# Two transformer layers on one core: down weights loaded ahead of the next block, GpSimd's bias rows in the projection, VectorE's weight halves in the last batch

## The chip, the cores and the metric

The kernel runs on one core of a Trainium2 chip. The metric is the time of one execution on the device in microseconds, as the median of several runs; less is better. The engines are TensorE (PE, matmul, with its weight loads as PEld), VectorE (DVE), ScalarE (ACT), GpSimd (POOL) and SyncE (SP), which here only issues DMAs. Each has a queue of its own and works it off in order; they wait for each other through semaphores.

## What is computed

Two layers on a residual x of 8 x 112 rows of 512, in fp32. Layer 0, which the change touches:

```python
x = layer_norm(hidden, ln1_w, ln1_b)
q, k, v = heads(x @ q_w + q_b), heads(ctx @ k_w + k_b), heads(ctx @ v_w + v_b)   # 16 heads of 32
attn = softmax(where(mask, q @ k.T / sqrt(32), min))      # 112 x 375 per batch and head
hidden = hidden + (attn @ v) @ cproj_w + cproj_b
out = hidden + gelu(layer_norm(hidden, ln2_w, ln2_b) @ fc_w + fc_b) @ proj_w + proj_b   # 512 -> 2048 -> 512
```

Layer 1 has two cross attentions with 16 heads of 128 and one more key each, and an MLP of the same size. The context has 8 x 375 rows of 512.

## The kernel before, in words

**Precision.** Every fp32 operand of a product is held as two halves, hi (ScalarE or VectorE writes it in fp32r) and lo (the difference, by a subtraction on VectorE or GpSimd). `product` makes three matmuls: hi x hi, hi x lo, lo x hi (lines 1696 to 1698).

**Weights** come in blocks of 512 x 512 in two slots, a and b. `load_block` on SP asks for four columns of 128 into `w_raw`; a column waits until the lo half of the same column of the block before is made (`w_lo`). `split_hi` (ScalarE, L877) makes hi, `split_lo` (L1234 on VectorE, L787 on GpSimd) makes lo. Slot a holds in turn the query weights, the key weights (A_K0) and the MLP's up weights (A_M0, A_M0 + 1, ...); slot b the value weights, the output projection (B_O0), and the MLP's down weights (B_M0, ...).

**Order of layer 0** (`schedule`, the same order on every engine):
- `ln(0)` and `query`: 896 rows are 7 tiles of 128. VectorE measures a row tile (`measure`, bn_stats L1238), normalizes it (`normalized`, L1263), TensorE turns it (`turn_row`, L1706), ScalarE scales it (`scaled`, L892), VectorE makes its halves (`halves`, L1269 and L1271). The query product is eight steps; steps 0 to 3 need the first four row tiles, and row tiles 4, 5 and 6 are turned behind steps 0, 1 and 2 (`later_rows`). Steps 4 to 7 need all seven. ScalarE evicts each step (L932).
- `attend_first`: eight batches, each of four tiles t of 128 columns, which are four heads j. For a tile: key product into ps_k (`key`), its eviction in two halves (`key_hi` L962, `key_lo` L1374), scores of four heads (`score_quad`, L1807), masked maximum (L1391), exp (L972), normalization (L1365, L1368), transpose (`turn`, L1820), eviction (`turned`, L968), weighted sum (`weighted`, L1832). Tile t + 1 is scored while tile t is turned. The parts of the following key and value products stand between the transposes (FILL). GpSimd makes the lo halves of the context for the batch after next (`context_lo`, L809), and then adds the output projection's bias to one row tile of x (`add_bias`, L803), for batches 0 to 6; it waits for nothing else between.
- In the last batch (`final`) there is no following batch. TensorE puts the first output rows (`first_row`) between the transposes; ScalarE makes the hi halves of B_O0 after each exp of tile 0, GpSimd their lo halves, and one column of A_M0 is made after each of tiles 0, 1 and 2. SP asks for A_M0 + 1, all four columns, and then for B_M0.
- `project`: last output rows, second layer norm (`add_y` L1574 adds a product to x). The last column of A_M0 is made here.
- `mlp`, four blocks: `up` in two chunks of four products with GELU (L1197), then `down`. In block 0 ScalarE also makes B_M0's hi halves and the halves of the context by key (L1188), which SP asked for behind B_M0 in `project`.

## Time and profile before

| | us |
|---|---|
| median of 3 runs (2320.42 to 2322.63) | 2320.61 |
| the profiled execution | 2322.78 |
| its span | 2321.0 |
| TensorE busy | 2276.6 (98%) |
| VectorE busy | 1335.5 (58%) |
| ScalarE busy | 1122.4 (48%) |
| GpSimd busy | 362.6 (16%) |
| mean granted TensorE clock, share of full | 0.999 |

A timeline row has the start in us from the span's start, the duration, the engine, line, operation, the tile written <- the tiles read, shapes, and the number of instructions merged into it. A bracket at its end is idle time of the engine just before it, and what ended that. PE's ends are modelled and its matmuls overlap, so a wait is read from the bracket, not from the gap. Layer 0's attention ends at about 297 us, its MLP at about 475 us.

### The profile page before, as it was taken

Reading aid. Unit: us, or ns where it says so; the run is one execution under the profiler, and the core shown is the slowest. Engines: PE = TensorE matmul, PEld = TensorE weight load, DVE = VectorE, ACT = ScalarE, POOL = GpSimd, SP = SyncE. Lnnn points to the kernel's source line nnn. Section 1 sums busy time; section 2 is a strip of 40 time slices with the busy share of each in tenths; the row PEclk is TensorE's granted clock in tenths of the full one; section 3 lists DMA queues with packets and bytes.
Section 4 is the critical chain, followed back from the end, with each engine's and each line's share of the span. In section 5 each row is a group of like instructions: output and inputs, shape, how many; then the busy total and the mean of one; then the engine's idle time right before and its main releaser. Section 6 shows DMA issues by size and latency. Waiting matters only on the chain.

```text
span 2321.0 us, 37085 instructions
## 1 busy us (share of the span) xinstructions
PE 2276.6 (98%) x13091; PEld 2068.1 (89%) x13091; DVE 1335.5 (58%) x3098; ACT 1122.4 (48%) x2468; POOL 362.6 (16%) x731
## 2 busy tenths in 40 slices
PE   7999999999999999999999999999999999999999
PEld 6777778899999999999998899999999999988888
DVE  5888764434655655655654525565565565554743
ACT  5777743344444445444543435445445444453421
POOL 1111045520000100100101210001001001003421
PEclk9999999999999999999999999999999999999999
DMA  6422036585545645654645564555555556444110
GB/s 192 139 90 98 16 117 197 183 251 152 190 144 194 226 168 170 226 190 151 236 144 158 179 190 153 197 177 189 198 197 177 197 190 201 173 156 136 58 55 32
DMA packets 255224, 376.25 MB, mean 162 GB/s; under 512 B 90302, under 2 KB 210514, under 8 KB 255042
## 3 DMA queue, kind: packets, MB, share of 16 engines
q1 hardware_dynamic: 255042, 373.87, 47.9%
q8 instruction: 108, 1.77, 0.3%
q14 instruction: 74, 0.61, 0.1%
HBM read 315.77 MB, written 58.05 MB: 161 GB/s over the span
## 4 chain that ended last, share of the span: by engine, by line
PE 92%; DVE 3%; ACT 2%; issue 2%; DMA 1%; SPq 0%; DVEq 0%; ACTq 0%
PE ps_k L1696 10%; PE ps_k L1697 10%; PE ps_k L1698 10%; PE ps_o L1696 9%; PE ps_o L1698 8%; PE ps_o L1697 8%; PE ps_v L1696 6%; PE ps_v L1698 6%; PE ps_v L1697 6%; PE ps_s L1696 4%; PE ps_s L1698 4%; PE ps_s L1697 4%; PE ps_t L1882 3%; PE ps_t L1820 2%; PE ps_o L1832 1%
## 5 line engine op out<-in xcount | busy, mean ns | idle before, releaser
L1696 PE MATMUL ps_k<-cs_hi,w_a_hi 128*128 128x376 f32 x1136 | 383.8, 338 | 2.8 <-DVE k_lo L1374 1.5
L1697 PE MATMUL ps_k<-cs_lo,w_a_hi 128*128 128x376 f32 x1136 | 379.5, 334 | 0.0
L1698 PE MATMUL ps_k<-cs_hi,w_a_lo 128*128 128x376 f32 x1136 | 378.5, 333 | 0.0
L1088 ACT ACTIVATE prob<-ps_s,row_columns 112x376 f32<-112x376 f32 x256 | 147.2, 575 | 303.5 <-DVE row_columns L1471 303.5
L829 POOL CAST k_hi<-xk_hi 128x1 fp32r<-128x1 f32 x256 | 47.0, 183 | 1232.4 <-PE ps_s L1698 1232.4
L1696 PEld LDWEIGHTS ps_k<-cs_hi,w_a_hi 128*128 128x128 f32 x1136 | 213.4, 188 | 4.7 <-issue 4.0
L1697 PEld LDWEIGHTS ps_k<-cs_lo,w_a_hi 128*128 128x128 f32 x1136 | 213.7, 188 | 0.5
L1698 PEld LDWEIGHTS ps_k<-cs_hi,w_a_lo 128*128 128x128 f32 x1136 | 213.6, 188 | 0.0
L1465 DVE SCALAR_TENSOR_TENSOR k_lo<-ps_k,col_b,k_hi 128x375 fp32r<-128x375 f32 x252 | 152.8, 606 | 75.0 <-ACT k_hi L1057 69.3
L1057 ACT ACTIVATE k_hi<-ps_k,col_b 128x375 fp32r<-128x375 f32 x252 | 143.9, 571 | 86.4 <-PE ps_k L1698 85.3
L1365 DVE RECIPROCAL row_columns<-row_columns 112x1 f32<-112x1 f32 x384 | 62.6, 163 | 197.9 <-ACT prob L1088 188.3
L1368 DVE TENSOR_SCALAR prob<-prob,row_columns 112x375 f32<-112x375 f32 x384 | 170.7, 445 | 4.5
L787 POOL TENSOR_TENSOR w_b_lo<-w_raw_b,w_b_hi 128x512 fp32r<-128x512 f32 x84 | 112.4, 1365 | 389.5 <-ACT w_b_hi L877 389.5
L1493 DVE TENSOR_TENSOR sums_lo<-ps_o,sums_hi 128x448 fp32r<-128x448 f32 x128 | 79.9, 624 | 131.6 <-ACT sums_hi L1071 131.6
L1471 DVE TENSOR_REDUCE row_columns<-ps_s 112x1 f32<-112x376 f32 x256 | 138.3, 540 | 8.0 <-PE ps_s L1698 8.0
L1698 PE MATMUL ps_v<-pt_hi,ckd_lo 128*128 128x448 f32 (+1 forms) x384 | 141.2, 368 | 0.0
L1696 PE MATMUL ps_v<-pt_hi,ckd_hi 128*128 128x448 f32 (+1 forms) x384 | 140.2, 365 | 0.9 <-DVE pt_lo L1487 0.9
L1698 PE MATMUL ps_o<-pt_hi,ckd_lo 128*128 128x448 f32 (+1 forms) x384 | 140.7, 366 | 0.0
L1696 PE MATMUL ps_o<-pt_hi,ckd_hi 128*128 128x448 f32 (+1 forms) x384 | 140.6, 366 | 0.0
L1697 PE MATMUL ps_v<-pt_lo,ckd_hi 128*128 128x448 f32 (+1 forms) x384 | 140.3, 365 | 0.0
L1697 PE MATMUL ps_o<-pt_lo,ckd_hi 128*128 128x448 f32 (+1 forms) x384 | 140.2, 365 | 0.0
L1493 DVE TENSOR_TENSOR sums_lo<-ps_v,sums_hi 128x448 fp32r<-128x448 f32 x128 | 80.0, 625 | 101.2 <-ACT sums_hi L1071 100.8
(275 smaller groups left out, 5712.3 us busy)
## 6 DMA issues: line engine op xcount, KB each, us to landing
ckd_hi<-context_by_key_halves SPq DMA_DIRECT2D x64, 768.0 KB, 4.4
ckd_lo<-context_by_key_halves SPq DMA_DIRECT2D x64, 768.0 KB, 6.2
cs_hi<-context_halves SPq DMA_DIRECT2D x64, 752.0 KB, 6.1
cs_lo<-context_halves SPq DMA_DIRECT2D x64, 752.0 KB, 7.8
w_raw_b<-in_blocks_b SPq DMA_DIRECT2D x104, 256.0 KB, 4.3
w_raw_a<-in_blocks_a SPq DMA_DIRECT2D x104, 256.0 KB, 4.8
q<-q_scratch SPq DMA_DIRECT2D x72, 224.0 KB, 6.0
extra<-extra_probability SPq DMA_DIRECT2D x16, 896.0 KB, 5.2
```

The lines of the kernel that those rows point to most:

```text
L787: pool.tensor_tensor(w[slot][1][:, :, part], w_raw[slot][:, :, part], w[slot][0][:, :, part], ALU.subtract).then_inc(w_lo[slot], 1)
L1057: act.activation(k[t % 2][0][:, 0:LK], key_bank(place, t)[:, 0:LK], ACT.Identity, bias=col_b[:, ds(place.column((C_BK0, C_BK1), t), 1)]).t ...
L1088: act.activation(prob[buf][0:LQ, 0:KW], ps_s[buf][0:LQ, 0:KW], ACT.Exp, bias=max_neg[0:LQ, buf:buf + 1], accum_out=prob_sum[0:LQ, buf:buf ...
L1365: dve.reciprocal(prob_rcp[0:LQ, col:col + 1], prob_sum[0:LQ, col:col + 1]).then_inc(s_rcp, 1)
L1368: dve.tensor_scalar(p[0:LQ, 0:LK], p[0:LQ, 0:LK], prob_rcp[0:LQ, col:col + 1], None, ALU.mult).then_inc(s_norm, 1)
L1465: dve.scalar_tensor_tensor(out=k[t % 2][1][:, 0:LK], in0=key_bank(place, t)[:, 0:LK], scalar=col_b[:, ds(place.column((C_BK0, C_BK1), t), 1)],
L1471: dve.tensor_reduce(max_neg[0:LQ, t % 2:t % 2 + 1], ps_s[t % 2][0:LQ, 0:KW], AX_X, ALU.max, negate=True).then_inc(s_max, 1)
L1493: dve.tensor_tensor(sums[1][:, d, cols], ps_c[d % 2][:, 0:HALF], sums[0][:, d, cols], ALU.subtract).then_inc(c_lo, 1)
L1696: pe.matmul(out, w_h, m_h, start=first, stop=False)
L1697: pe.matmul(out, w_h, m_l, start=False, stop=False)
L1698: return pe.matmul(out, w_l, m_h, start=False, stop=last)
L1882: last = pe.transpose(ps_t[buf][0:n, i * LQ:(i + 1) * LQ], prob[buf][0:LQ, k0:k0 + n], ident[0:LQ, 0:LQ])
```

## The change

- `key_bank`: in layer 0, tile 1 of the first batch goes to ps_o[0] in place of ps_k.
- `ln(0)`: GpSimd adds the bias to row tiles 0 to 3 when four row tiles have their halves, and to 4 to 6 when row tile 6 is normalized, and then makes batch 1's context halves. `attend_first` adds none. Row tile 6 is turned behind query step 1; its deviation on ScalarE stands ahead of the first query eviction; VectorE normalizes it ahead of row 4's halves.
- Last batch: the hi halves of B_O0 stand at other places on ScalarE, VectorE makes the lo halves, and the columns of A_M0 are made in tiles 2 and 3.
- `project`: row 6 is added and measured ahead of row 4's halves.
- SP: B_M0 is asked for in the last batch with nothing ahead of it; three columns of A_M0 + 1 stand behind the first context by key, the fourth behind the next bias row.

```diff
+PROJECTION_LOW = {(0, 1): 0, (1, 0): 2, (1, 1): 3}
...
         self.key_ahead = 2 if layer == 0 else 3
-        self.split_slots_b = {(NB - 1, 0): range(4)} if layer == 0 else {}
...
-    def split_columns_b(self, t):
...
-        return self.att.split_slots_b.get((self.b, t), ()) if isinstance(self.b, int) else ()
...
+if not place.att.layer:
+    return ps_o[0] if place.head and place.parity == 0 and t == 1 else ps_k
...
-return place.att.layer and place.head and (t == NT - 1 if place.parity == 0 else t < NT - 1)
+if not place.att.layer:
+    return place.head and place.parity == 0 and t == 1
+return place.head and (t == NT - 1 if place.parity == 0 else t < NT - 1)
...
 if isinstance(norm, int) and norm == 0:
-    return {0: (4,), 1: (5,), 2: (6,)}
+    return {0: (4,), 1: (5, 6)}
...
     sp.sem_inc(sp_waited, 1)
+    if isinstance(e, int) and e == 1:
+        load_block(0, A_M0 + 1, [3])
...
         if place.swap:
-            load_block(0, place.block_a + 2)
...
         load_by_key_raw(0)
+        load_block(0, A_M0 + 1, range(3))
...
+    if isinstance(e, int) and e == 0:
+        pool.wait_ge(bias_in, 16)
+        pool.wait_ge(ln_lo, 4)
+        for r in range(4):
+            add_bias(r)
+        pool.wait_ge(ln_xhat, RT)
+        for r in range(4, RT):
+            add_bias(r)
+        context_lo(Place(ATT0, 0, 0, 0, 1))
+        return
     pool.wait_ge(ln_lo, RT * e + RT)
-    if has_pending(e):
-        split_lo(*pending(e)[0:2])
-    if isinstance(e, int) and e == 0:
-        context_lo(Place(ATT0, 0, 0, 0, 1))
+    split_lo(*pending(e)[0:2])
     pool.wait_ge(bias_in, 16 * e + 16)
-    if has_pending(e):
-        for r in range(RT):
-            add_bias(r)
+    for r in range(RT):
+        add_bias(r)
...
         for t in range(NT):
-            if t == 0 and place.b < RT:
-                add_bias(place.b)
...
                 context_lo(place.after(2))
-            split_lo(1, place.block_b + 1, place.split_columns_b(t))
...
         deviation(0, 5)
+        deviation(0, 6)
...
             scaled(norm, row)
-        if not layer and i == 0:
-            deviation(0, 6)
...
         act.sem_inc(act_waited, 1)
-        act.activation(k[t % 2][0][:], ps_k[:, 0:KW], ACT.Identity,
+        act.activation(k[t % 2][0][:], key_bank(place, t)[:, 0:KW], ACT.Identity,
...
+    def projection_part(place, s):
+        split_hi(1, place.block_b + 1, [s], lambda s: (v_mm, 3 * place.batch + 3))
...
+    def mlp_part(place, s):
+        split_hi(0, place.block_a + 1, [s], lambda s: (k_mm, place.tile + NT))
...
         following = place.key(t + 1)
-        for j in range(SUB0):
-            if not (t == 0 and j == 3):
-                turned(place, t, j)
-            if t == 0 and j == 2:
-                turned(place, t, 3)
-            if following:
-                exp(*following, j)
-            if key_evicted(place, t, j):
-                key_hi(*key_evicted(place, t, j))
-            if t == 0:
-                split_hi(1, place.block_b + 1, (j,), lambda s: (v_mm, 3 * place.batch + 3))
-            if t == NT - 1 and j == 1:
-                deviation(1, 0)
-                deviation(1, 1)
-        if t == NT - 1:
+        turned(place, t, 0)
+        if t == 0:
+            projection_part(place, 0)
+            exp(*following, 0)
+            turned(place, t, 1)
+            exp(*following, 1)
+            turned(place, t, 2)
+            turned(place, t, 3)
+            exp(*following, 2)
+            key_hi(*place.key(t + 2))
+            exp(*following, 3)
+            projection_part(place, 1)
+        if t == 1:
+            projection_part(place, 2)
+            exp(*following, 0)
+            turned(place, t, 1)
+            projection_part(place, 3)
+            exp(*following, 1)
+            turned(place, t, 2)
+            exp(*following, 2)
+            key_hi(*place.key(t + 2))
+            turned(place, t, 3)
+            exp(*following, 3)
+        if t == 2:
+            exp(*following, 0)
+            turned(place, t, 1)
+            exp(*following, 1)
+            mlp_part(place, 0)
+            turned(place, t, 2)
+            exp(*following, 2)
+            turned(place, t, 3)
+            exp(*following, 3)
+            mlp_part(place, 1)
+        if t == 3:
+            mlp_part(place, 2)
+            turned(place, t, 1)
+            deviation(1, 0)
+            deviation(1, 1)
+            turned(place, t, 2)
+            turned(place, t, 3)
...
             output_hi(place, t)
-            if place.split_column(t) is not None and not (place.final and t == NT - 1):
+            if place.split_column(t) is not None and not place.final:
...
         measure_rows((6,))
+        scale_rows((6,))
         halves(0, 4)
-        scale_rows((6,))
...
         dve.wait_ge(k_hi, place.tile + t + 1)
-        dve.scalar_tensor_tensor(out=k[t % 2][1][:], in0=ps_k[:, 0:KW], scalar=col_a[:, C_BK0 + t:C_BK0 + t + 1],
+        dve.scalar_tensor_tensor(out=k[t % 2][1][:], in0=key_bank(place, t)[:, 0:KW], scalar=col_a[:, C_BK0 + t:C_BK0 + t + 1],
...
             measure(1, r)
+        split_lo(0, A_M0, [2])
...
                         key_lo(*place.key(t + 2))
+                if place.final and (t, j) in PROJECTION_LOW:
+                    split_lo(1, place.block_b + 1, [PROJECTION_LOW[t, j]])
+                if place.final and (t, j) == (2, 1):
+                    split_lo(0, place.block_a + 1, [0])
...
                 normalized_0(*following, SUB0 - 1)
+            if place.final and t == 0:
+                split_lo(1, place.block_b + 1, [1])
+            if place.final and t == 2:
+                split_lo(0, place.block_a + 1, [1])
...
             output_lo(place, t)
-            if place.split_column(t) is not None and not (place.final and t == NT - 1):
+            if place.split_column(t) is not None and not place.final:
...
         measure(norm, 5)
+        add_y(6, 0, 0)
+        scale(5)
+        measure(norm, 6)
         halves(norm, 4)
-        scale(5)
-        add_y(6, 0, 0)
-        measure(norm, 6)
+        scale(6)
         split_lo(0, A_M0, [3])
-        scale(6)
...
         if two_key_banks(place, t) and place.parity == 0:
-            pe.wait_ge(q_act, 8 * (4 * place.a + 4) + 6)
+            pe.wait_ge(q_act, 8 * (4 * place.a + 4) + 6 if place.att.layer else 7)
```

## Rows read from the trace of the kernel before

**Rows 1.** The page: busy us (share of the span) x instructions of each engine
```profile
PE 2276.6 (98%) x13091; PEld 2068.1 (89%) x13091; DVE 1335.5 (58%) x3098; ACT 1122.4 (48%) x2468; POOL 362.6 (16%) x731
```

**Rows 2.** Timeline, query projection: start, us, engine, line, operation, count [idle before <-releaser]
```profile
27.03 0.69 DVE L1271 TENSOR_TENSOR act_t_lo<-o,act_t_hi 128x512 fp32r<-128x512 f32 x1
...
29.82 0.55 DVE L1263 TENSOR_SCALAR shared<-x,mean_var,row_columns 128x512 f32<-128x512 f32 x1
...
30.93 0.69 DVE L1238 BATCH_NORM_STATS2 stats<-x 128x6 f32<-128x512 f32 x1
...
31.23 1.50 ACT L892 ACTIVATE o<-ps_t,col_a 128x128 f32<-128x128 f32 x4
...
33.69 0.45 PE L1696 MATMUL ps_o<-act_t_hi,w_a_hi 128*128 128x448 f32 x1
...
40.22 0.47 PE L1696 MATMUL ps_k<-act_t_hi,w_a_hi 128*128 128x448 f32 x1 [1.03 <-DVE act_t_lo L1271]
```

**Rows 3.** Timeline, first MLP block, where GpSimd adds the second bias
```profile
327.60 8.88 POOL L803 TENSOR_TENSOR x<-x,bias_row 128x512 f32<-128x512 f32 x6
...
332.41 1.53 DVE L1648 TENSOR_TENSOR cs_lo<-prob,cs_hi 128x384 fp32r<-128x384 f32 x1
```

**Rows 4.** Timeline, PE at the start of attention
```profile
53.63 0.41 PE L1696 MATMUL ps_k<-cs_hi,w_a_hi 128*128 128x376 f32 x1 [1.49 <-DVE k_lo L1374]
```

**Rows 5.** Timeline, batch 1's last tile and its fellows in other batches
```profile
107.59 3.15 POOL L809 TENSOR_TENSOR cs_lo<-ctx_raw,cs_hi 128x376 fp32r<-128x376 f32 x3
...
110.71 1.28 POOL L803 TENSOR_TENSOR x<-x,bias_row 128x512 f32<-128x512 f32 x1
...
110.98 1.22 DVE L1368 TENSOR_SCALAR prob<-prob,row_columns 112x375 f32<-112x375 f32 x1
...
114.04 0.61 ACT L972 ACTIVATE prob<-prob,row_columns 112x375 f32<-112x375 f32 x1 [1.40 <-DVE row_columns L1391]
...
115.22 0.49 PE L1820 MATMUL ps_t<-ident,prob 112*128 112x112 f32 x3 [0.67 <-ACT shared L968]
...
85.62 0.48 PE L1820 MATMUL ps_t<-ident,prob 112*128 112x112 f32 x3 [1.19 <-ACT shared L968]
...
257.03 0.42 DVE L1368 TENSOR_SCALAR prob<-prob,row_columns 112x375 f32<-112x375 f32 x1
```

**Rows 6.** Timeline, the last batch
```profile
267.10 1.47 DVE L1368 TENSOR_SCALAR prob<-prob,row_columns 112x375 f32<-112x375 f32 x1
...
273.85 0.68 DVE L1234 TENSOR_TENSOR w_a_lo<-w_raw_a,w_a_hi 128x512 fp32r<-128x512 f32 x1
...
269.27 0.79 PE L1832 MATMUL ps_o<-shared,v 128*32 128x112 f32 x24 [1.30 <-ACT shared L968]
...
271.06 0.42 PE L1807 MATMUL ps_s<-k_hi,q 32*112 32x376 f32 x2 [1.00 <-DVE k_lo L1374]
...
276.20 0.49 PE L1820 MATMUL ps_t<-ident,prob 112*128 112x112 f32 x3 [1.52 <-ACT shared L968]
```

**Rows 7.** Timeline, SP's queue and the MLP's first products
```profile
274.55 37.97 SPq L531 DMA_DIRECT2D w_raw_a<-in_blocks_a  x4
...
309.78 0.66 PE L1706 MATMUL ps_t<-ident,shared 128*128 128x128 f32 x4 [0.32 <-DVE shared L1263]
...
313.94 0.47 PE L1696 MATMUL ps_s<-act_t_hi,w_a_hi 128*128 128x512 f32 x1 [0.30 <-ACT prob L1197]
...
322.75 0.63 ACT L1188 ACTIVATE ckd_hi<-ctx_raw 128x512 fp32r<-128x512 f32 x1 [0.74 <-DMA ctx_raw<-in_ctx_by_key]
...
324.10 0.42 PE L1696 MATMUL ps_s<-act_t_hi,w_a_hi 128*128 128x384 f32 x1 [2.34 <-ACT prob L1197]
```

**Rows 8.** Busy us by stretch: PE, PEld, DVE, ACT, POOL, PEclk, DMA share, GB/s
```profile
325.00:326.00 1.00, 1.00 (x5) 1.00 (x4) 0.14 (x1) 1.00 (x3) 1.00 (x1) 0.50 0.62 150
...
325.00:330.00 5.00, 5.00 (x23) 5.00 (x22) 3.38 (x5) 2.60 (x5) 5.00 (x4) 0.70 0.58 163
...
1220.00:1222.00 2.00, 2.00 (x7) 1.78 (x6) 0.00 (x0) 0.32 (x1) 0.00 (x0) 0.50 0.92 330
```

## The prediction

> **What bounds the kernel now.** I read the page's head first: TensorE is busy in 2276.6 us, 98% of the span of 2321.0 [rows 1]. So there are at most 44 us of idle TensorE in the whole kernel, and the change can win only where TensorE waits; work moved between the other engines counts only through such a wait. Next I went down TensorE's timeline from 0 to 560 us and kept the rows that end in a bracket, that is those with idle time ahead of them: 32 rows, some 33 us, of which 10.4 is the first load. For each wait in a stretch that the diff touches I then read VectorE, ScalarE, GpSimd and SP's queue backwards from the releaser, since the bracket names only the last link. Last I looked at the granted clock by stretch: it is 1.00 (2.4 GHz) but for two places, where it is 0.50, the lower level of 1.2 GHz [rows 8]; both stand right behind waits of TensorE.
>
> The profiled execution took 2322.78 us, 2.17 more than the median of 2320.61. I make the sum against the profiled one and come back to the difference.
>
> **1. Key tile 1 of the first batch gets its own bank (gain 1.5).** TensorE waits 1.49 us for the low half of tile 0, only because both tiles use ps_k [rows 4]. With tile 1 in ps_o[0] the product starts at once. The new wait, for the seventh query product's eviction, ends before it, as products 5 to 8 are evicted as they come. Next late is the score of tile 0, which needs the same low half; the 12 matmuls of tile 1's product, some 2 us, now lie above it. The rest of the start hangs on TensorE and moves along. Bounds 1.0 and 1.5.
>
> **2. GpSimd's bias rows leave the batches (gain 4.2).** In batches 0 to 5 there is one wait each before a transpose in the last tile: 1.19 us once and about 0.68 five times [rows 5]. The chain behind the 0.67 is: the context's low halves hold GpSimd until 107.59 + 3.15 = 110.74, a bias row follows at 110.71 for 1.28. VectorE's normalization issued at 110.98 takes 1.22, and the same instruction takes 0.42 in batch 6, where GpSimd is idle. It ends 0.2 behind the end of the bias row. So the maximum that follows, ScalarE's exp (which idles 1.40 for it), the eviction behind the exp and TensorE's transpose are all 0.80 late. Without the row 0.80 goes, and 0.67 of it is TensorE's. Five times 0.67 and 0.83 (0.80 to 0.83 of the 1.19; the rest, 0.36, has other reasons) make 4.2. What is late next is TensorE itself: the eviction ahead of the transpose is then done about 0.1 us before it is wanted, which is thin. The other slowed normalizations lie under the context halves, which stay. Bounds 0 (the 0.1 doesn't hold) and 4.6.
>
> **3. The same rows now run in the projection (loss 1.3).** This is the edit that I am least sure of. GpSimd begins rows 0 to 3 when the fourth row's low half is done, 27.03 + 0.69, and rows 4 to 6 when row 6 is normalized. In that stretch VectorE is on the path: TensorE starts its fifth product at 40.22, after waiting 1.03 for VectorE's last halves [rows 2]. In the other stretch where GpSimd adds a bias, its rows take 8.88 / 6 = 1.48 each, and VectorE's subtraction takes 1.53 [rows 3], against 0.69 for a wider one alone [rows 2]: about one VectorE operation per GpSimd row. First without contention: ScalarE now does row 6's deviation ahead of the first query eviction, so it waits for statistics that start at 30.93 and are aggregated by about 31.95; its scaling of row 4 moves from 31.23 to about 32.85 and ends at 34.35. TensorE turns row 6 one product earlier, where the third product now starts, at 33.69, but that turn waits for row 4's scaling: 0.7 lost, 1.03 won, because the last halves are then done at about 39.0. With contention the normalizations of rows 4 and 5 (29.82 and the next) each wait for the end of a bias row, which puts the statistics of row 6 1.2 later; the turn waits 1.9; and three casts and three subtractions for rows 4 to 6 meet the bias rows 4 to 6. I get the last halves at about 41.4, 1.3 later, and TensorE's fifth product at 41.5 in place of 40.22: a loss of 1.3. Bounds: a gain of 1.0 (nothing is put in), and a loss of 4 (a whole further row of 1.28 ahead of two of the halves). I take 1.3, as rows 3 are the same operations on the same engines.
>
> The Trainium skill says the same of the cause (SBUF — State Buffer, Who interferes with whom): VectorE and GpSimd share one port pair as an exclusive lock, and an instruction with two SBUF inputs or in a 2-port mode is fully blocked. By that rule bn_stats, with one input, would not wait, and edit 3 stays as worked out; by a lock on every VectorE instruction the statistics would wait too and it would come out about 1.3 higher. No row shows statistics beside a GpSimd row. It is the rule that speaks against this edit.
>
> **4. The last batch (gain 0.9).** TensorE waits 1.30, 1.00 and 1.52 there, 3.8 in all [rows 6]. The cause is again GpSimd, which makes four weight halves while VectorE's normalizations take 1.47 (against 0.42 in rows 5). VectorE now makes those halves itself, four at about 0.6 of its queue each (0.68 in rows 6); one more, of the MLP's weights, leaves the first tile. Going through the new order with these durations: ScalarE has one half ahead of its evictions in place of two, so the weighted sum starts at about 268.6 (was 269.27); the third tile's low half is done about 0.4 earlier, scores at 270.65 (was 271.06). Then the fourth weight half is ready only at about 275.5, and the first output row, which now comes up at 274.5, has to wait about 1 us for it; before, it was covered by the wait of 1.52. At the end of tile 1 TensorE is 1.0 ahead. In tiles 2 and 3 one more MLP half comes before the third row's addition; about 0.1 is given back. Bounds 0 and 3.8; a loss is not to be had unless the fourth half is later than 276.4.
>
> **5. Order of rows 5 and 6 ahead of the MLP (gain 0.6).** VectorE now adds row 6 and measures it before row 4's halves. Row 5's normalization is done some 0.4 earlier and takes the wait of 0.32; row 6's deviation comes 1.1 earlier, so does ScalarE's table load and first GELU behind it, which takes the 0.30 [rows 7]. The row 4 halves that are moved back are wanted only by the second chunk. Bounds 0 and 0.6.
>
> **6. Loads (gain 2.3, and 1.5 of clock).** SP's queue stands from 274.55 on the fourth column of MLP block 1, for 37.97 us [rows 7], since that column waits for VectorE's last weight half of the block before, made only behind the output rows. Behind it stand the down weights and the by-key context. ScalarE waits for both, in order, until 322.75, with the GELU that TensorE needs behind them: 2.34 us at 324.10. After the change the down weights and the context are asked for at about 273 to 276, and land some 40 us before their use. The column that was in the way now comes behind the bias row. ScalarE's two pairs of weight halves then follow GELUs 3 and 4, done before TensorE asks; so nothing takes the place of the 2.34. Behind this wait the clock fell to 0.50, and from 325 to 330 us its mean is 0.70 [rows 8]: TensorE is busy all of these 5 us, so 0.30 x 5 = 1.5 is lost. Bounds 2.3 and 3.9.
>
> **The sum.** -1.5 -4.2 +1.3 -0.9 -0.6 -2.3 -1.5 = -9.7 on 2322.78, so 2313.1. The median run is 2.17 shorter, about what one of the two slow-clock stretches costs, so it may have only one of them. I count half of the 1.5 for the median: -9.0 on 2320.61 = **2311.6 us**. Everything behind the first MLP waits on TensorE and only moves along.
>
> **The rivals.**
> (a) The rows are free in the projection: no contention, edit 3 is a gain of 0.4. For it: VectorE has gaps between rows 4 and 6, while it waits for ScalarE. Against it: rows 3. Time 2311.6 - 1.7 = 2309.9, and to 2308 if the last batch wins more than I work out.
> (b) The batches' wait has a second cause 0.1 us behind, such as ScalarE's order or the context halves, and edit 2 gives only 1.2. For it: the thin margin. Against it: batch 6 has no such wait and no GpSimd work. Time 2311.6 + 3.0 = 2314.6.
> (c) The loads do not do what they say: ScalarE is held by something else in the first MLP block, and edit 6 gives nothing. Time 2311.6 + 3.1 = 2314.7. Against it: no other instruction stands between those evictions.
> (d) Slower: the port lock only changes its place. Each of the seven rows, 1.28 us, stands whole in the way of VectorE's chain in the projection (9.0), TensorE's wait there brings a stretch at the lower clock (1.5, as in edit 6), and edit 2 gives nothing as in (b). Then 9.0 + 1.5 - 1.5 - 0.9 - 0.6 - 3.1 = +4.4: 2325.0. It decides from a loss of about 6 us in the projection. Against it: TensorE's products there leave only 1.03 of wait, and most VectorE work on rows 4 to 6 starts after rows 0 to 3 are done.
>
> **Chances.** Forecast 0.58, (a) 0.16, (b) 0.13, (c) 0.08, (d) 0.05. The range goes from 2307.5 (a, with more from the last batch) to 2316.0 (b or c with the upper bound of edit 3): what is left out is (d) and the ends. A measurement of this kernel can tell 0.2%, 4.6 us, from no change. The forecast, (a) and nearly all of (b) and (c) are faster than that, below 2316.0: 0.88. Within it lie the worst of (b), (c) and half of (d): 0.09. Slower 0.03.
>
> **What would show it.** Edit 1: no wait before the second key tile. Edit 2: no GpSimd bias rows after 50 us, a normalization of 0.42 at the old place, and batches 1 to 5 shorter by 0.7 each. Edit 3: GpSimd rows at 28 to 33 and 34 to 39 us, VectorE rows of 1 us and more among them, a new TensorE wait of 1 to 2 us before the turn of row 6, and the fifth product at about 41.5; if it starts at 39.5, (a) holds. Edit 4: a wait of about 1 us before the first output row. Edit 6: no wait on a DMA by ScalarE in the MLP and clock 1.00 from 320 to 330 us. I am wrong if the batches keep their length, or if TensorE's idle time in the projection exceeds 4 us.

## The result, and the profile after

Six runs of the changed kernel have a median of 2310.32 us (2309.29 to 2311.28), six of the kernel before in the same comparison 2321.62 us (2319.28 to 2323.83). The ratio is 0.9952, 95% interval 0.9939 to 0.9964: faster by 0.48%, 11.3 us. The forecast was 2311.6 us in a range of 2307.5 to 2316.0. The profiled execution took 2311.28 us, its span is 2309.5, against 2322.78 and 2321.0 before.

The head of the page after: engine, busy us (share of the span), instructions.
```profile
PE 2273.7 (98%) x13091; PEld 2066.5 (89%) x13091; DVE 1340.2 (58%) x3102; ACT 1123.7 (49%) x2468; POOL 360.5 (16%) x727
```
Against [rows 1], TensorE's work is the same and its busy time 2.9 us less, GpSimd has four instructions fewer and VectorE four more (the weight halves of edit 4). Most of the gain was idle time of TensorE.

So I went by marks on TensorE's timeline that both kernels have, and took the time between them. In us:

| stretch (from the start of ... to ...) | before | after | change | forecast |
|---|---|---|---|---|
| first to fifth query product (edit 3) | 12.45 | 13.09 | +0.64 | +1.3 |
| first key product to next value product (edit 1) | 6.64 | 4.93 | -1.71 | -1.5 |
| batches 0 to 5, each up to its last weighted sum, the first from that value product (edit 2) | | | -4.9 (0.79 to 0.85 each) | -4.2 |
| last batch, to the first up product (edit 4) | 43.46 | 43.37 | -0.09 | -0.9 |
| up, first chunk (edit 5) | 13.08 | 12.13 | -0.95 | -0.6 |
| up, second chunk, to the first down product (edit 6) | 12.47 | 9.14 | -3.33 | -3.8 |

The column sums to -10.3 (forecast -9.7); 0.27 more come from the start: the first query product stands at 27.77 before and at 27.50 after, and between 26.92 and 28.05 in the ten profiles of this document. Behind the first MLP both kernels do the same; the end is 11.5 us earlier, with the stretch at the lower clock near 1220 us, worth 1.7, that the profile after lacks. So some 0.8 is given back on the way; 0.6 of it stands here:
```profile
527.04 0.58 ACT L960 ACTIVATE q<-q 128x448 fp32r<-128x448 f32 x1 [2.26 <-DMA q<-q_scratch]
...
528.95 0.41 PE L1742 MATMUL ps_k<-cs_hi,w_a_hi 128*128 128x376 f32 x1 [0.47 <-DVE k_lo L1511]
```
ScalarE waits 2.26 for a load of layer 1's queries there (1.57 before), and TensorE for what comes behind it. Before the change, and in e1, e4, e5 and e7, TensorE has no such wait; in e2, e3, e6 and e8 it is 0.16 to 0.52. It goes with none of the edits, as far as these profiles tell.

Timeline of the kernel after, query projection: start, us, engine, line, operation, count, [idle before <-releaser].
```profile
27.62 5.39 POOL L813 TENSOR_TENSOR x<-x,bias_row 128x512 f32<-128x512 f32 x4 [27.18 <-DVE act_t_lo L1308]
...
29.53 0.92 DVE L1300 TENSOR_SCALAR shared<-x,mean_var,row_columns 128x512 f32<-128x512 f32 x1
...
30.56 1.31 DVE L1300 TENSOR_SCALAR shared<-x,mean_var,row_columns 128x512 f32<-128x512 f32 x1
31.79 0.68 DVE L1275 BATCH_NORM_STATS2 stats<-x 128x6 f32<-128x512 f32 x1
...
35.65 1.66 DVE L1308 TENSOR_TENSOR act_t_lo<-o,act_t_hi 128x512 fp32r<-128x512 f32 x1
37.23 1.52 DVE L1306 CAST act_t_hi<-o 128x512 fp32r<-128x512 f32 x1
38.78 0.69 DVE L1308 TENSOR_TENSOR act_t_lo<-o,act_t_hi 128x512 fp32r<-128x512 f32 x1
```
```profile
30.50 0.66 PE L1752 MATMUL ps_t<-ident,shared 128*128 128x128 f32 x4 [0.32 <-DVE shared L1300]
35.23 0.63 PE L1752 MATMUL ps_t<-ident,shared 128*128 128x128 f32 x4 [1.22 <-issue]
```
GpSimd's rows run from 27.6 to 33.0 and from 34.1 on. Two normalizations, one cast and one subtraction stretch beside them (0.55 to 0.92 and 1.31, 0.43 to 1.52, 0.69 to 1.66). TensorE pays with the 1.22 before row 6's turn; the 1.03 before the fifth product [rows 2] is gone. The statistics at 31.79 lie beside GpSimd's fourth row and keep their 0.68.

TensorE in the last batch and in the MLP's up product, kernel after; these are all its waits between 262 and 452 us:
```profile
262.33 0.79 PE L1878 MATMUL ps_o<-shared,v 128*32 128x112 f32 x24 [0.68 <-ACT shared L974]
264.23 0.42 PE L1853 MATMUL ps_s<-k_hi,q 32*112 32x376 f32 x2 [1.12 <-DVE k_lo L1411]
270.13 0.50 PE L1742 MATMUL ps_v<-w_b_hi,act_t_hi 128*128 128x512 f32 x1 [0.41 <-DVE w_b_lo L1271]
286.90 0.47 PE L1742 MATMUL ps_v<-w_b_hi,act_t_hi 128*128 128x512 f32 x1 [0.37 <-DVE x L1620]
300.11 0.51 PE L1742 MATMUL ps_s<-act_t_hi,w_a_hi 128*128 128x512 f32 x1 [1.19 <-DVE act_t_lo L1308]
319.22 0.42 PE L1742 MATMUL ps_s<-act_t_hi,w_a_hi 128*128 128x384 f32 x1 [0.58 <-ACT prob L1234]
```
Of the 2.34 in [rows 7] a new wait of 0.58 is left, and the releaser is no longer held by a DMA. Why, VectorE's, GpSimd's and ScalarE's timelines of the same stretch say:
```profile
311.43 6.42 POOL L791 TENSOR_TENSOR w_b_lo<-w_raw_b,w_b_hi 128x512 fp32r<-128x512 f32 x4 [88.78 <-ACT w_b_hi L884]
```
```profile
311.40 0.69 DVE L1694 TENSOR_TENSOR cs_lo<-prob,cs_hi 128x512 fp32r<-128x512 f32 x1
312.01 1.53 DVE L1692 CAST cs_hi<-prob 128x512 fp32r<-128x512 f32 x1
313.57 1.67 DVE L1694 TENSOR_TENSOR cs_lo<-prob,cs_hi 128x512 fp32r<-128x512 f32 x1
```
```profile
318.50 0.58 ACT L1234 ACTIVATE prob<-ps_s,col_a 128x384 f32<-128x384 f32 x1 [2.04 <-DVE q L1694]
```
The weights come earlier now, so GpSimd starts their low halves at 311.43 in place of 321.63, and VectorE's halves of the hidden rows take 1.5 to 1.7 each beside them. ScalarE's GELU waits 2.04 for them.

The granted clock by stretch, kernel after: window, its length, busy of PE (x), PEld, DVE, ACT, POOL, then the clock, DMA share and GB/s. Of all stretches of 5 us in which TensorE works, the first is the only one below 1.00 (but for 0.96 in the last, at the span's end).
```profile
265.00:270.00 5.00, 4.72 (x23) 4.43 (x21) 3.79 (x12) 3.30 (x9) 0.00 (x0) 0.66 0.36 104
320.00:325.00 5.00, 5.00 (x25) 4.39 (x25) 4.97 (x4) 1.75 (x4) 5.00 (x4) 1.00 0.07 21
325.00:330.00 5.00, 5.00 (x23) 4.13 (x22) 4.93 (x4) 2.54 (x5) 5.00 (x5) 1.00 0.00 0
```
The 0.70 from 325 to 330 [rows 8] is gone. But now the clock is 0.66 from 265 to 270 us, that is at its lower level (1.2 GHz) for part of it, right behind the waits of 0.68 and 1.12: 0.34 x 5 = 1.7 us of the last batch.

### The profile page after: what moved, and what is told of

The parts are those of the page before. It is cut to its first block, busy times and chain, and to the rows that moved or that the text cites. A ratio compares the mean times of both kernels' runs of the same rounds, so it can differ in the third digit from the quotient of the medians.

```text
span 2309.5 us, 37085 instructions
## 1 busy us (share of the span) xinstructions
PE 2273.7 (98%) x13091; PEld 2066.5 (89%) x13091; DVE 1340.2 (58%) x3102; ACT 1123.7 (49%) x2468; POOL 360.5 (16%) x727
## 4 chain that ended last, share of the span: by engine, by line
PE 92%; DVE 4%; ACT 2%; issue 1%; DMA 1%; POOL 0%; SPq 0%; DVEq 0%; ACTq 0%
PE ps_k L1742 10%; PE ps_k L1743 10%; PE ps_k L1744 10%; PE ps_o L1742 9%; PE ps_o L1744 8%; PE ps_o L1743 8%; PE ps_v L1742 6%; PE ps_v L1744 6%; PE ps_v L1743 6%; PE ps_s L1742 4%; PE ps_s L1744 4%; PE ps_s L1743 4%; PE ps_t L1928 3%; PE ps_t L1866 2%; PE ps_s L1853 1%
## 5 line engine op out<-in xcount | busy, mean ns | idle before, releaser
L1405 DVE TENSOR_SCALAR prob<-prob,row_columns 112x375 f32<-112x375 f32 x384 | 162.8, 424 | 4.5
L1108 ACT ACTIVATE sums_hi<-ps_o 128x448 fp32r<-128x448 f32 x128 | 69.8, 545 | 141.2 <-PE ps_o L1744 141.0
```

Source lines behind the costliest of these rows:

```text
L1108: act.activation(sums[0][:, d, place.quarter * HALF:(place.quarter + 1) * HALF], ps_c[d % 2][:, 0:HALF], ACT.Identity).then_inc(c_hi, 1)
L1405: dve.tensor_scalar(p[0:LQ, 0:LK], p[0:LQ, 0:LK], prob_rcp[0:LQ, col:col + 1], None, ALU.mult).then_inc(s_norm, 1)
```

## The experiments

Theory: each edit works through its own wait of TensorE, and the times add. Rivals: the batches' gain is not GpSimd's rows alone; the loads alone bring less; the rows cost nothing in the projection; the last batch's edit does nothing but move the lower clock. The kernel before had 2321.16 us (median of 19 runs) beside e1 to e4, and 2321.32 (of 10) beside e5 to e8.

### e1: edit 6 alone, on the kernel before

```diff
+                if isinstance(e, int) and e == 1:
+                    load_block(0, A_M0 + 1, [3])
...
-                        load_block(0, place.block_a + 2)
...
+                    load_block(0, A_M0 + 1, range(3))
```


> The kernel before with the order of the loads alone changed (down weights with nothing ahead of them, three columns of the next up block behind the context by key, the fourth behind the bias row). Theory: ScalarE no longer waits on a DMA in the first MLP block; the stretch from the second chunk's first product to the first down product goes from 12.47 us to about 9.1 (2.34 of wait and about 1.5 of slow clock less, 0.5 given back by VectorE's halves beside GpSimd), and the median falls by 2.0 to 3.4 us. Rival: something else holds ScalarE there and the stretch stays at 12 us or more. Second rival: all 3.9 us go and nothing is given back, 8.6 us.

Measured: 2318.69 us, ratio 0.999 (0.998 to 1.000); the second chunk of the up product takes 9.35 us in place of 12.47. TensorE's wait there:
```profile
326.37 0.41 PE L1698 MATMUL ps_s<-act_t_hi,w_a_hi 128*128 128x384 f32 x1 [0.78 <-ACT prob L1199]
```
What follows: the loads alone give 3.1 us in this stretch (9.1 was expected, 9.35 came), so rival (c) falls. The medians are 2.5 apart, as expected. The new wait behind VectorE's halves belongs to this edit, as it is here too. The lower clock left the MLP with the wait, but this run has it from 270 to 275 us (0.66), where it costs nothing: the wait of 1.52 in [rows 6] is gone in it, and the last batch takes 43.48 us in place of 43.46.

### e2: edit 2 and, of edit 3, the rows alone, on the kernel before

```diff
                     for t in range(NT):
-                        if t == 0 and place.b < RT:
-                            add_bias(place.b)
```
with `ln` of GpSimd as in the changed kernel.

> The kernel before with GpSimd's seven bias rows moved from the batches to the projection, and nothing else. Theory (the bias row blocks VectorE's normalization): each of batches 0 to 5 gets 0.8 us shorter, 4.9 us from the start of attention to the first weighted sum of batch 6, and the wait before the transpose is gone; the projection loses, as VectorE's normalizations and halves stand beside GpSimd's rows: the fifth query product starts 0.8 to 1.5 us later than before (40.22). Together 3.4 to 4.1 us less. Rival: the batches' waits were shortened by other edits (the second key bank, the other order of rows): the batches stay within 0.2 us.

Measured: 2319.62 us, ratio 0.9992 (0.9982 to 1.0001). From the first key product to batch 6 it takes 187.65 us in place of 192.52, 4.87 less. The projection loses 1.45:
```profile
40.82 0.47 PE L1700 MATMUL ps_k<-act_t_hi,w_a_hi 128*128 128x448 f32 x1 [2.13 <-DVE act_t_lo L1275]
```
What follows: the batches' whole gain comes from this edit, without help from the others. In the old order of the projection the price shows before the fifth product (2.13 in place of 1.03). The two stretches together give 3.4, the low end of what was expected; the medians give only 1.5, with an interval that includes no change, so the median doesn't show this gain by itself.

### e3: the changed kernel without the seven bias rows

GpSimd does not add the bias to x in layer 0's first stage; the output projection's bias is missing from the result. In both loops over r:
```diff
-                        add_bias(r)
+                        pool.sem_inc(bias_add, 1)
```


> The changed kernel without GpSimd's seven bias rows (the layer 0 projection bias is left out of the sum, so the output isn't the reference's). Theory of the lock: the two normalizations of 0.92 and 1.31 us beside the rows go back to 0.55, row 6's turn waits 0.6 to 0.8 us in place of 1.22, and the fifth query product starts at 39.6 to 39.9 in place of 40.59: the rows' price is 0.7 to 1.0 us. Rival, the order on ScalarE alone (row 6's deviation ahead of the first eviction) makes the wait: the fifth product stays at 40.4 or later. The rest of the kernel unchanged.

Measured: 2309.57 us, ratio 0.9949. The projection stretch takes 11.87 us: 1.22 less than in the changed kernel and 0.58 less than before.

TensorE's wait before row 6's turn is 0.46 in place of 1.22:
```profile
33.99 0.63 PE L1752 MATMUL ps_t<-ident,shared 128*128 128x128 f32 x4 [0.46 <-issue]
```
What follows: the new order of ScalarE's and VectorE's work in the projection is a gain of 0.58, and the rows cost 1.22 on top, more than the 0.7 to 1.0 that I expected. This turn starts 6.60 us behind the first query product, against 7.73 in the changed kernel (35.23 - 27.50): 1.13 of the 1.22 is there already. It comes from the two normalizations; the slow cast and the slow subtraction behind it add at most 0.1. So rival (a) falls, and so does the size of both halves of my step 3 (1.0 and 2.3).

### e4: three bias rows behind the last low half, four behind the context's

```diff
-                    pool.wait_ge(ln_lo, 4)
-                    for r in range(4):
+                    pool.wait_ge(ln_lo, RT)
+                    for r in range(3):
                         add_bias(r)
-                    pool.wait_ge(ln_xhat, RT)
-                    for r in range(4, RT):
-                        add_bias(r)
                     context_lo(Place(ATT0, 0, 0, 0, 1))
+                    for r in range(3, RT):
+                        add_bias(r)
```


> The changed kernel with the same seven bias rows later: three after all of the projection's halves are made, then batch 1's context halves, then four. Theory: the projection is as without the rows (fifth product at 39.6 to 39.9), the rows run from 39 to 53 us beside little VectorE work, and the kernel is 0.7 to 1.0 us shorter than the changed one, about 2309.5 where that one has 2310.3. Rival: the lock only moves; VectorE's query and key halves at 52 to 54 us wait for a row, the first scores come late by 0.5 to 1.3 us, and the gain is gone.

Measured: 2310.05 us, ratio 0.995 (0.9935 to 0.9965). The projection takes 11.87 us, as without the rows, and the start of attention 4.93, as in the changed kernel.
```profile
39.23 4.33 POOL L812 TENSOR_TENSOR x<-x,bias_row 128x512 f32<-128x512 f32 x3 [38.79 <-DVE act_t_lo L1307]
```
The other four run from 48.28 to 54.16, and VectorE's query half beside them takes 1.52, against 0.63 in the changed kernel:
```profile
48.28 5.88 POOL L812 TENSOR_TENSOR x<-x,bias_row 128x512 f32<-128x512 f32 x4
51.48 1.52 DVE L1396 TENSOR_TENSOR q<-q 128x448 fp32r<-128x448 f32 x1 [1.37 <-ACT q L959]
```
What follows: the price of edit 3 is one of place, not of work. Three rows start at 39.23, when VectorE's last half is done; the other four do stretch VectorE's work, as the rival said, but TensorE doesn't wait for it, and none of the seven costs anything. At the end of the first MLP this kernel is 0.94 us ahead of the changed one, though its first query product came 0.55 later. The medians (2310.05 and 2310.32) can't tell the two apart; the profiled run has a second stretch at the lower clock, at 2050 to 2060 us, worth 0.35 x 5 = 1.75.

### e5: edit 1 undone

```diff
-                return ps_o[0] if place.head and place.parity == 0 and t == 1 else ps_k
+                return ps_k
...
-                return place.head and place.parity == 0 and t == 1
+                return False
```


> The changed kernel with edit 1 undone: the second key tile of the first batch shares the bank ps_k again. My theory: only the stretch from the first key product to the next value product changes, from 4.93 us back to about 6.6, and everything behind it is 1.5 to 1.7 us later, so about 2311.9 beside 2310.3. Rival: the rows' move made VectorE late at the start of attention as well, then the wait before the second key tile is longer than the 1.49 us of the kernel before. A second rival: something behind the start takes the gain back, then batch 0 or 1 is shorter here than in the changed kernel.

Measured: 2313.03 us, ratio 0.9964 (0.995 to 0.9978).
```profile
53.92 0.41 PE L1742 MATMUL ps_k<-cs_hi,w_a_hi 128*128 128x376 f32 x1 [1.49 <-DVE k_lo L1411]
```
The wait of [rows 4] is back with the same 1.49, the stretch takes 6.64 us in place of 4.93, and TensorE stays 1.6 to 1.7 later than in the changed kernel from there to the end of batch 6. Both rivals fall. The median is 2.7 above the changed kernel's, where 1.6 was expected; the 1.7 rests on the stretches.

Then something I had not planned: between the last weighted sum of batch 6 and the second of batch 7 this kernel gains 1.2 on the changed one. Its clock is 1.00 there:
```profile
265.00:270.00 5.00, 4.00 (x33) 3.35 (x33) 4.71 (x15) 4.30 (x12) 0.00 (x0) 1.00 0.35 103
270.00:275.00 5.00, 4.49 (x51) 3.43 (x51) 3.46 (x12) 3.29 (x10) 0.00 (x0) 1.00 0.80 270
```
So it shows what edit 4 does without the lower clock: last batch to first up product 42.17 us (42.14 in e8, at full clock too), against 43.46 before.

### e6: GpSimd makes the output projection's low halves again

```diff
-                            if place.final and (t, j) in PROJECTION_LOW:
-                                split_lo(1, place.block_b + 1, [PROJECTION_LOW[t, j]])
...
-                        if place.final and t == 0:
-                            split_lo(1, place.block_b + 1, [1])
```
and in GpSimd's program, behind its loop over t:
```diff
+                        if place.final and t == 0:
+                            split_lo(1, place.block_b + 1)
```


> The changed kernel with GpSimd making the output projection's four low halves in the last batch, as before (VectorE's other new work of that batch stays). My theory: VectorE's normalizations there take 1.2 to 1.5 us again beside GpSimd, and the wait before the weighted sum of tile 0 is 1.3 instead of 0.7 us; from the end of batch 6 to the first MLP product (43.4 us in the changed kernel, with one stretch at the lower clock in it that costs 1.7) it takes 43.4 to 44.5, whichever of the two has the slow clock. Rival: edit 4 did nothing but bring the slow clock into this stretch, then this kernel takes 41.7 to 42 there and beats the changed one by 1.5 us.

Measured: 2311.94 us, ratio 0.9959 (0.9944 to 0.9974). The stretch takes 44.46 us, with 0.66 of clock from 270 to 275.
```profile
262.10 0.79 PE L1876 MATMUL ps_o<-shared,v 128*32 128x112 f32 x24 [0.68 <-ACT shared L976]
263.75 0.43 PE L1851 MATMUL ps_s<-k_hi,q 32*112 32x376 f32 x2 [0.87 <-DVE k_lo L1413]
267.66 0.49 PE L1864 MATMUL ps_t<-ident,prob 112*128 112x112 f32 x3 [0.31 <-ACT shared L976]
269.43 0.50 PE L1740 MATMUL ps_v<-w_b_hi,act_t_hi 128*128 128x512 f32 x1 [1.28 <-POOL w_b_lo L791]
```
What follows: TensorE is busy for all of 270 to 280 in this run, so its 1.7 of lower clock count in full, and it would take 42.76 at full clock; e5 takes 42.17. The rival (42 or less, without edit 4's low clock) falls. By these single profiles, and with the clock taken off, moving the halves to VectorE is worth about 0.6 of edit 4's 1.3; the other 0.7 is the new order of ScalarE's and VectorE's work. One detail of my expectation was wrong: the wait before the weighted sum stays 0.68. In the kernel before, ScalarE works without a gap from 265.79 to the eviction that this sum waits for, with the second of two weight halves just ahead of the last evictions:
```profile
267.84 0.61 ACT L877 ACTIVATE w_b_hi<-w_raw_b 128x512 fp32r<-128x512 f32 x1
268.36 0.43 ACT L968 ACTIVATE shared<-ps_t 128x336 f32<-128x336 f32 x1
268.69 0.44 ACT L968 ACTIVATE shared<-ps_v 128x336 f32<-128x336 f32 x1
```
So the 1.30 of [rows 6] came from ScalarE's order and not from GpSimd. (In e6 GpSimd's halves also come at other times, as ScalarE's do, and the normalization at this place takes 0.41.) What GpSimd's halves cost here is the wait for the fourth of them (1.28 in place of 0.67 in e5).

### e7: the bias rows back in the batches

```diff
+                        if t == 0 and place.b < RT:
+                            add_bias(place.b)
```
with the rows taken out of GpSimd's `ln(0)` in the changed kernel.

> The changed kernel with GpSimd's seven bias rows put back into the batches. My theory: batches 0 to 5 take 29.3 us again in place of 28.5, together 4.9 more, while the projection up to the fifth product is 1.2 us shorter, as in the run without the rows (11.87 in place of 13.09 us). So +3.7 at the first MLP, about 2314.0. Rival: the bank of edit 1 or the weight halves of edit 4 had a part in the batches' gain; then the batches come back by less than 4.5 us.

Measured: 2313.96 us, ratio 0.997 (0.9958 to 0.9982). The median is 3.6 above the changed kernel's, as expected. Batches 0 to 5 take 4.88 us more, 0.77 to 0.87 each; the projection takes 11.87. TensorE is 3.67 us later at the first MLP, counted from the first query product (+3.7 was expected).
```profile
112.27 0.49 PE L1863 MATMUL ps_t<-ident,prob 112*128 112x112 f32 x3 [0.68 <-ACT shared L971]
```
What follows: the 0.67 of [rows 5] come back with the rows, and nothing of the batches' gain belongs to another edit.

### e8: GpSimd's down-weight halves begin behind VectorE's third hidden half

The order of e4, and in GpSimd's `ln(1)`:
```diff
                 pool.wait_ge(ln_lo, RT * e + RT)
+                if isinstance(e, int) and e == 1:
+                    pool.wait_ge(h_lo, 3)
                 split_lo(*pending(e)[0:2])
```


> The changed kernel with the rows' order of e4, and with GpSimd's down-weight halves at the first MLP begun only when VectorE has made the third of its hidden halves. My theory of what edit 6 lacks of its 3.8: the new wait of 0.58 us before the second chunk's third product comes from VectorE's hidden halves, slowed to 1.5 to 1.7 each beside GpSimd; here the third pair takes 1.1 in place of 3.2, the wait is gone, and the second chunk to the first down product takes 8.6 in place of 9.14 us, about 0.5 us in the total, too little to see in the median. Rival: the halves come too late for the down products then (four of 1.6 us from about 313.2 end at 319.6, down starts at 319.9), or the bias rows, 1.7 us later, hold up the additions: the stretch is 9.1 or more.

Measured: 2309.35 us (2308.75 to 2310.06), ratio 0.9948 (0.9933 to 0.9963), the fastest median of all, though not apart from the changed kernel's 0.9952. GpSimd and VectorE in its profile:
```profile
310.65 6.19 POOL L791 TENSOR_TENSOR w_b_lo<-w_raw_b,w_b_hi 128x512 fp32r<-128x512 f32 x4 [89.44 <-DVE cs_lo L1695]
```
```profile
309.38 0.42 DVE L1693 CAST cs_hi<-prob 128x512 fp32r<-128x512 f32 x1
309.83 0.69 DVE L1695 TENSOR_TENSOR cs_lo<-prob,cs_hi 128x512 fp32r<-128x512 f32 x1
310.62 0.43 DVE L1693 CAST q<-prob 128x512 fp32r<-128x512 f32 x1
311.08 1.67 DVE L1695 TENSOR_TENSOR q<-prob,q 128x512 fp32r<-128x512 f32 x1
```
The third pair takes 1.1 us in place of 3.2, TensorE has no wait between 297.46 and the first down product, and the second chunk takes 8.32 us (8.6 was expected, 9.14 in the changed kernel). The additions behind it don't slow: the end of the first MLP is earlier by the same 0.8. The rival falls. The clock is 1.00 in the last batch here too; the one low stretch is at 2050 to 2055.

## Why the prediction was right, step by step

**The time.** 2311.6 was predicted, 2310.3 measured: right sign, 1.3 us too cautious. The gains of edits 1, 2 and 5 were put too small and the loss of edit 3 too large; those of 4 and 6 were put too large, as the profile has them. The errors partly cancel, and that the total came so near is in part luck.

**Edit 1**, forecast -1.5, measured -1.71 and confirmed by undoing it (e5). The mechanism is as told. I took the bracket (1.49) as the price of the wait, and the stretch is 1.71.

**Edit 2**, forecast -4.2, measured -4.9, twice more in e2 and e7. The chain GpSimd row, normalization, exp, eviction, transpose is right: in the kernel after GpSimd ends its context halves at 108.6 and the normalization at the old place (108.82) takes 0.41. The mis-sized term is TensorE's share: I worked out that the chain is 0.80 earlier and then counted only the bracket's 0.67; each batch got 0.79 to 0.85. Rival (b), a second cause 0.1 us behind, is refuted: e2 and e7 move the rows alone, and the whole comes and goes.

**Both are one error.** The bracket is less than these waits cost. In the batches 0.67 stands for 0.80, in the start 1.49 for 1.71, before the MLP 0.32 + 0.30 for 0.95 (edit 5), and 0.58 for 0.82 (e8): 0.13 to 0.24 per wait. The rows show why. In [rows 5] the matmul ahead of the transpose starts at 114.21 and is given 0.34, so the bracket of 0.67 is counted from 114.55. But TensorE starts the next instruction before the last one's end where nothing holds it. The same two in the kernel after:
```profile
112.04 0.33 PE L1744 MATMUL ps_k<-cs_hi,w_a_lo 128*128 128x376 f32 x1
112.25 0.49 PE L1866 MATMUL ps_t<-ident,prob 112*128 112x112 f32 x3
```
They start 0.21 apart, against 1.01 before: 0.80 less, which is what each batch got.

**Edit 3**, forecast +1.3, measured +0.64: the step I was least sure of, right in sign, half in size. I had a gain of 1.0 from the order and a loss of 2.3 from contention; e3 gives 0.58 and 1.22. The duration that I took for a VectorE operation beside a row holds (1.52 and 1.66 for the cast and the subtraction, 1.53 in [rows 3]), and so does the first half of the loss: the normalizations put the turn of row 6 1.2 later by my working, 1.13 by e3. The mis-sized term is the second half, 1.1 more from the halves. I let three casts and three subtractions meet the rows, and only one of each did, as GpSimd's last three rows were done by 38.5; they cost 0.1. The profile showed what I listed for this step: rows at 27.6 to 33 and from 34.1, a new wait before row 6's turn (1.22). The fifth product started 13.09 us behind the first; I had put 13.7 (41.5 - 27.77).

The Trainium skill (SBUF — State Buffer, Who interferes with whom) says that VectorE and GpSimd lock each other out where VectorE's instruction reads two SBUF inputs or runs in a 2-port mode. By that rule bn_stats, with one input, should not wait, and here it didn't: 0.68 at 31.79 beside a GpSimd row, 0.69 alone [rows 2]. That bounds the loss, as I had assumed. I also wrote that no row shows statistics beside a GpSimd row. The kernel before has such rows, at the end of the first MLP, so this could have been read before the run:
```profile
458.23 5.33 POOL L787 TENSOR_TENSOR w_a_lo<-w_raw_a,w_a_hi 128x512 fp32r<-128x512 f32 x4 [8.11 <-ACT w_a_hi L877]
462.74 0.69 DVE L1238 BATCH_NORM_STATS2 stats<-x 128x6 f32<-128x512 f32 x1
```

**Edit 4**, forecast -0.9, measured -0.09 in this profile and -1.29 in e5, at full clock. The terms: the weighted sum's wait went from 1.30 to 0.68, as told, though through ScalarE's order and not GpSimd; the scores, which I had 0.4 earlier, came 0.60 earlier counted from batch 6's end, with a wait of 1.12 in place of 1.00; the wait before the first output row, put at 1, is 0.67 (e5) or 0.41. What I left out is that a stretch at the lower clock can fall behind the waits that remain there. It costs 1.7 in rows and 1.2 net (43.37 against 42.17), in part because the wait behind it shrinks from 0.67 to 0.41. It is not shown to be edit 4's doing: e1, whose last batch is that of the kernel before, has such a stretch there too.

**Edit 5**, forecast -0.6, measured -0.95. Both waits are gone as told; the rest is the bracket again.

**Edit 6**, forecast -2.3 and -1.5 of clock, measured -3.33. With no wait and full clock this stretch takes 8.32 (e8). Before it had 12.47, 4.15 more: 2.34 of wait and 0.05 x 5 + 0.30 x 5 = 1.75 of clock make 4.09. So both causes are confirmed. I wrote that nothing takes the place of the 2.34. That sentence was wrong: with the weights early, GpSimd's halves fall on VectorE's, and 0.82 is given back.

**The clock.** I counted the MLP's low stretch as won. It was (1.00 from 320 to 330 in e1, e3 to e8 and the kernel after), but six of these eight profiles have one in the last batch instead. A profile is one execution, though, and executions of one kernel differ. The record has the mean clock of each, rounded to 0.001; one stretch of 1.7 us makes it 0.999. It is 1.000 in four of the six executions of the changed kernel (2309.29 to 2310.40) and 0.999 in the two slowest, one of which is the profiled one. Of the kernel before, 4 of the 29 executions beside e1 to e8 have 1.000. So the changed kernel's median has no low stretch at all, and edit 4 is worth its 1.3 there. Comparing only executions with 1.000, the kernels are 9.5 us apart, so the clock's share of the 11.3 is about 1.8 (an estimate from these few). I had put 0.75 for it, half of 1.5, by a guess, and 8.2 for all the rest.

**Rival (d)**, slower, needed a loss of 6 us in the projection; it lost 0.6. **Rival (a)** is nearer in time (2309.9, against my 2311.6) and wrong in its cause: e3 shows the rows' price.

**What stays open.** What decides whether and where the clock falls. The kernel before, e1 and e2 have the same code and nearly the same waits in the last batch (1.30, 1.00), and only e1's profile is low there; the changed kernel, e3, e4 and e7 are low there, e5 and e8 are not, all with 0.68 and 1.11 or 1.12. As executions of one kernel differ too, one profile of each can't tell. Nor is it explained why the load of layer 1's queries comes later in some profiles.

## What to carry to other kernels

Where the bottleneck engine waits for a chain that another pair of engines stretches, move the intruding work to a place where the victim's last step is done or where the bottleneck doesn't wait for it, not only out of the hot loop: the same seven rows cost 4.9 us in the batches, 1.2 in the projection and nothing when they began 11 us later (e4). Work through what an earlier load will trigger: it starts the next engine's work earlier too, and that may fall on a neighbour. And price a removed wait from start to start of the instructions around it, not by the bracket, which here was 0.13 to 0.24 us short where both could be read.

## What the runs showed that I had not expected

- The lower clock is not bound to the wait that one removes. All ten profiles, counted in stretches of 5 us over the whole span but its last 10 us:

| kernel | span | stretches below 1.00 | us lost in them |
|---|---|---|---|
| before | 2321.0 | 320 to 330, 1215 to 1225 | 1.75 + 1.70 |
| e2, rows alone | 2316.5 | 315 to 325 | 1.75 |
| e1, loads alone | 2316.6 | 270 to 275 | 1.70 |
| after | 2309.5 | 265 to 270 | 1.70 |
| e3, no rows | 2308.3 | 260 to 270 | 1.70 |
| e4, rows late | 2309.8 | 260 to 270, 2050 to 2060 | 1.70 + 1.75 |
| e5, one bank | 2309.2 | none | 0 |
| e6, GpSimd's halves | 2311.4 | 270 to 275 | 1.70 |
| e7, rows back | 2313.0 | 265 to 275 | 1.70 |
| e8, halves wait | 2307.0 | 2050 to 2055 | 1.70 |

  (Lost is the sum of one less the clock, times 5.) One stretch is worth 1.7 us each time, a sixth of this change. With them taken off, the spans are 2317.6 before and 2307.8 after, 9.8 apart. Each row is one execution; the table doesn't rank the kernels.
- A stretch at the lower clock can cost nothing: in e1 it lies where TensorE would have waited 1.52 us behind it, and the stage is as long as before.
- VectorE's casts with one SBUF input and 512 columns take 1.4 to 1.5 us beside GpSimd where they take 0.42 alone (312.01 against 310.95 in the kernel after); the statistics, with one input too, take 0.68 in both.
